# Layernorm, attention and a routed two-expert MLP on one core: gathered rows turned by DVE from quarter loads instead of by PE, with earlier loads, a folded bias and another schedule of the sums

## The reference

```python
xn = layernorm(x)                        # x: 8 x 512 x 256, 4096 tokens of 256
scale = xn[:, ::128].reshape(8, 1024)    # four rows of the batch, a factor per key
attn = softmax((xn @ k.T) * scale) @ v   # 1024 keys, 256 wide
shared = gelu(xn @ Wfc_s + bfc_s) @ Wproj_s + bproj_s      # hidden 1024
gate = top-2 of softmax(xn @ Wr), renormalised             # 8 experts
routed = sum over the two experts of gate_e * (gelu(xn @ Wfc_e + bfc_e) @ Wproj_e + bproj_e)
out = x + attn + shared + routed
```

## Time and profile before

| | |
|---|---|
| median of 3 runs | 823.47 us (821.97 to 823.82) |
| the profiled execution | 822.49 us, of which the span of instructions is 820.6 us |
| PE busy | 777.3 us (95%) |
| DVE busy | 483.1 us (59%) |
| ACT busy | 440.5 us (54%) |
| POOL busy | 260.4 us (32%) |
| HBM traffic | 157 GB/s over the span |
| mean granted clock of PE | 0.988 of full speed |

### The profile page before, as it was taken

The page is one execution under the profiler, slowest core; times in us unless marked ns, Lnnn a source line. Parts: engine busy times, 40 slices in busy tenths (PEclk is TensorE's granted clock), DMA queues, the critical chain, the costliest instruction groups (busy, mean ns, idle before and its releaser), DMA issues.

```text
span 820.6 us, 21229 instructions
## 1 busy us (share of the span) xinstructions
PE 777.3 (95%) x7222; PEld 662.1 (81%) x7222; DVE 483.1 (59%) x1215; ACT 440.5 (54%) x845; POOL 260.4 (32%) x289
## 2 busy tenths in 40 slices
PE   4999999999999986979999999999999999999996
PEld 3888876767777665868999999989999999888885
DVE  6887858888887792653444344333444433436666
ACT  5655537665559753435655465444455554455551
POOL 5445425556656650662121111112112121110000
PEclk9999999999999997999999999999999999999999
DMA  9533222746566845444422355645454536304446
GB/s 296 193 128 104 84 73 78 259 154 232 203 209 227 332 187 193 131 135 122 158 73 65 116 174 162 203 131 161 160 167 123 191 118 205 100 26 138 125 150 213
DMA packets 65627, 129.29 MB, mean 158 GB/s; under 512 B 12256, under 2 KB 47408, under 8 KB 59168
## 3 DMA queue, kind: packets, MB, share of 16 engines
q1 hardware_dynamic: 59088, 110.77, 42.2%
q0 software_dynamic: 6480, 17.77, 5.7%
HBM read 88.39 MB, written 40.13 MB: 157 GB/s over the span
## 4 chain that ended last, share of the span: by engine, by line
PE 73%; DVE 13%; POOL 5%; issue 4%; DMA 3%; SPq 1%; DVEq 0%; ACT 0%; another core or an unknown queue 0%; POOLq 0%; ACTq 0%
PE ps_h L1321 30%; PE ps_v L1341 30%; PE ps_v L1461 5%; PE ps_h L1393 4%; POOL acc L637 3%; DVE xn L895 3%; PE ps_t L1257 2%; DVE prob L1018 2%; PE ps_t L1407 1%; DVE p_t L1032 1%; DMA tokens_y<-prob,to_i 1%; POOL slots_x L660 1%; DVE acc L1040 1%; DMA b_rows<-in_L_ffn_bfc_s_dram 1%; DVE x_t L845 1%
## 5 line engine op out<-in xcount | busy, mean ns | idle before, releaser
L944 DVE TENSOR_TENSOR h_split<-h,h_split 128x512 f16<-128x512 f32 (+1 forms) x224 | 151.5, 686 | 153.5 <-ACT h_split L751 152.8
L745 ACT ACTIVATE h<-ps_h,b_fc 128x256 f32<-128x256 f32 (+1 forms) x320 | 125.7, 443 | 181.7 <-PE ps_h L1321 181.6
L1321 PE MATMUL ps_h<-x_t,w_split 128*128 128x256 f16 (+1 forms) x1920 | 196.6, 263 | 7.3 <-DVE x_t L1134 7.3
L1321 PEld LDWEIGHTS ps_h<-x_t,w_split 128*128 128x128 f16 x1920 | 172.6, 99 | 26.0 <-issue 8.1
L1341 PE MATMUL ps_v<-w_stage,h_split 128*128 128x256 f16 x1704 | 192.6, 273 | 0.0
L1341 PEld LDWEIGHTS ps_v<-w_stage,h_split 128*128 128x128 f16 x1704 | 165.1, 98 | 18.5
L704 POOL DMA_INDIRECT tokens_y<-prob,to_i x71 | 72.0, 1015 | 309.1 <-DMA tokens_y<-prob,to_i 200.1
L751 ACT CAST h_split<-h 128x512 f16<-128x512 f32 (+1 forms) x224 | 130.7, 584 | 10.1
L745 ACT ACTIVATE h<-ps_h,b_t 128x256 f32<-128x256 f32 x128 | 53.4, 467 | 76.4 <-PE ps_h L1321 76.2
L1461 PE MATMUL ps_v<-v_split,p_t 128*128 128x256 f16 x768 | 90.9, 276 | 0.0
L1321 PE MATMUL ps_h<-x_t,w_shared 128*128 128x256 f16 x768 | 89.4, 278 | 0.0
(11 more groups left out here) (156 smaller groups left out, 665.4 us busy)
## 6 DMA issues: line engine op xcount, KB each, us to landing
w_split<-wpack SPq DMA_DIRECT2D x17, 1024.0 KB, 5.3
w_stage<-wpack SPq DMA_DIRECT2D x17, 1024.0 KB, 5.3
wpack<-w_split SPq DMA_DIRECT2D x8, 1024.0 KB
wpack<-h_split SPq DMA_DIRECT2D x8, 1024.0 KB, 5.0
y_rows<-tokens_y SPq DMA_DIRECT2D x32, 256.0 KB, 3.1
x_split<-slots_x SPq DMA_DIRECT2D x31, 258.0 KB
b_pj<-bias_e SPq DMA_DIRECT2D x40, 128.5 KB, 3.1
w_stage<-in_L_ffn_Wfc_dram SPq DMA_DIRECT2D x4, 1024.0 KB
```

The costliest lines, as they stand in the source:

```text
L745: ins = nc.scalar.activation(h32[:, hc, 0:n], ps_h[:, hc * TILE:hc * TILE + n], ACT.Gelu_apprx_tanh, bias=bias[:, hc:hc + 1], scale=1.0 / WS)
L944: ve.tensor_tensor(h_split[par][:, 1, 2 * b:2 * b + 2, 0:n], h32[:, 2 * b:2 * b + 2, 0:n], h_split[par][:, 0, 2 * b:2 * b + 2, 0:n], ALU.s ...
L1321: ins = mm(ps_h[:, hc * TILE:hc * TILE + cols], wv[:, wl, c, hc * P:(hc + 1) * P], x[:, xl * DC + c, 0:cols], start=n == 0, stop=n == 3 * ...
```

## The change

It has five parts. x_split's columns are written in another order (column 4f + k holds feature f of chunk k), by DVE's cast and subtraction through a strided view; PE's turning of the sixteen tiles reads them through the same view. In the routed stage SP loads a gathered tile in four quarters of 128 columns, each to 32 partitions (`x_quad`), and DVE turns 32x32 blocks straight into x_t (`turn_slots`); `tr2`, `tr2_first`, `copy_slots` and `keep_tail` are gone, and the routing columns come by a DMA of their own (`load_tail`). The first of these loads are issued in attention step 28, before the last packed weights are stored. The shared bias is added once to the eight expert rows at the start (b_both), and `add_bias` is gone. The lower half of the first weights' low part is made by DVE instead of POOL, and the sums are spread as five, five, five, five, four, four, four and none.

```diff
+QUADS = 4
+QW = ROW // QUADS
...
+        x_quad = [t[:, :, :].rearrange("p a n -> p (a n)")[:, 0:SUB * ROW].rearrange("p (t n) -> p t n", n=QW)
+                  for t in x_split[0:2]]
...
-        PER = QT // (SHARED - NA)
+        SUMS = (range(0, 5), range(5, 10), range(10, 15), range(15, 20), range(20, 24), range(24, 28), range(28, 32), ())
...
-            sp.dma_start(b_pj_s[:, :], bproj_s.partition_broadcast(P)).then_inc(s_bpj_in, 16)
+            sp.dma_start(b_pj_s[:, :], bproj_s.partition_broadcast(EXPERTS)).then_inc(s_bpj_in, 16)
+            sp.dma_start(b_both[:, 0:D], bproj).then_inc(s_bpj_in, 16)
...
+            def load_slots(j, par, half, first=False):
+
+                if not first:
+                    wait_ge(sp, s_xt2, j - 1)
+                r = sp.value_load(tab_x[0:1, ds(j, 1)], min_val=0, max_val=SPARE)
+                n = P if half else TILE
+                for qd in range(QUADS):
+                    src = slots_x[ds(r, n), qd * QW:(qd + 1) * QW].rearrange("(b t) f -> t b f", t=32)
+                    sp.dma_start(x_quad[par][qd * 32:(qd + 1) * 32, 0:n // 32, :], src).then_inc(s_xs_in[par], 16)
+
+            def load_tail(j, par, half, first=False):
...
-                sp.dma_start(dst, src).then_inc(s_xs_in[par], 16)
-
+                if u == 28:
+
+                    wait_ge(sp, s_table, TABLE)
+                    for par in range(2):
+                        wait_ge(sp, s_scat[par], 32 * SHARED)
+                    wait_ge(sp, s_pad, 16 * (EXPERTS + SUB))
+                    load_slots(0, 0, False, first=True)
+                    load_slots(1, 1, True, first=True)
+                    wait_ge(sp, s_bt_out, 16)
+                    for n in range(4):
+                        wait_ge(sp, s_w_out[n], 16 * (EXPERTS // 4))
+                    wait_ge(sp, s_w_out[0], 16 * (JOBS // 4))
+                    load_fc(0, 0, first=True)
+
+            wait_ge(sp, s_w_out[1], 16 * (JOBS // 4))
+            load_fc(1, 1, first=True)
...
-            wait_ge(pool, s_w0_hi[1], 1)
-            g.tensor_tensor(w_shared[0][:, 2048 + HID:], w_stage[0][:, HID:], w_shared[0][:, HID:2 * HID],
-                            ALU.subtract).then_inc(s_w0_lo[1], 1)
+            wait_ge(pool, s_bpj_in, 32)
+            g.tensor_tensor(b_both[:, 0:D], b_both[:, 0:D], b_pj_s[:, :], ALU.add).then_inc(s_bias, 1)
...
-            wait_ge(pool, s_bpj_in, 16)
-            wait_ge(pool, s_fin, QT)
-            for i in range(SHARED):
-                add_bias(i)
...
+            def x_half(i, hl):
+
+                return x_split[i % 3][:, :, 0:ROW].rearrange("p a (f h c) -> p h a c f", h=2, c=DC)[:, hl]
...
-                ve.tensor_copy(x_split[i % 3][:, :, 0:D], xn[par][:, :, :]).then_inc(s_hl, 1)
+                ve.tensor_copy(x_half(i, 0), by_quad(xn[par])).then_inc(s_hl, 1)
...
-                ve.tensor_tensor(x_split[i % 3][:, :, D:ROW], xn[par][:, :, :], x_split[i % 3][:, :, 0:D],
-                                 ALU.subtract).then_inc(s_hl, 1)
+                ve.tensor_tensor(x_half(i, 1), by_quad(xn[par]), x_half(i, 0), ALU.subtract).then_inc(s_hl, 1)
...
-            def copy_slots(j, par, n=TILE):
-                dve.wait_ge(s_tr2, j + 1)
+            def turn_slots(j, par, n=TILE):
+
+                dve.wait_ge(s_xs_in[par], nth(j, par, 16 * QUADS))
                 if not (isinstance(j, int) and j < 2):
-                    dve.wait_ge(s_to, j - 1)
-                keep_tail(par, n // P)
-                dve.wait_ge(s_mm1, BANKS * (R0 + j - 1))
-                ve.tensor_copy(x_t[:, par, :, 0:n], tr16[:, :].rearrange("p (c n) -> p c n", n=TILE)[:, :, 0:n]
-                               ).then_inc(s_xt2, 1)
+                    dve.wait_ge(s_mm1, BANKS * (R0 + j - 1))
+                ve.transpose(x_t[:, par, :, 0:n].rearrange("p c (b t) -> p b c t", t=32),
+                             x_quad[par][:, 0:n // 32, :].rearrange("p b (r c) -> p b c r", r=32)).then_inc(s_xt2, 1)
...
+                            chunk = src[:, a, 0:ROW].rearrange("p (f k) -> p k f", k=2 * DC)
+                            ins = nc.tensor.transpose(out[:, n:n + P],
+                                                      chunk[:, hl * DC + c, :], ident_h[:, :])
```

More of the change, by code:

```diff
@@ L457, in _ @@
                     load_job(2)
[L460 to L478, removed]
             def expert_of(j):
@@ new lines, in load_slots @@
+                for qd in range(QUADS):
[3 more added lines that the diff above has]
+                if not first:
+                    wait_ge(sp, s_to, j - 1)
+                r = sp.value_load(tab_x[0:1, ds(j, 1)], min_val=0, max_val=SPARE)
+                subs = 1 if half else SUB
+                sp.dma_start(tail[par][:, 0:subs, :].bitcast(f16),
+                             slots_x[ds(r, subs * P), ROW:].rearrange("(a p) d -> p a d", p=P)).then_inc(s_tail[par], 16)
@@ new lines, in _ @@
+            for u in range(QT):
+                k, phase = u // 3, u % 3
+                i = NA + 1 + k
+                if phase == 1 and i < SHARED:
+                    store_row(i)
+                if u == 0:
+                    load_job(3)
+                for n in range(JOBS):
+                    if u == lo_slot(n, 1) + 1:
+                        store_job(n)
+                        if n + 4 < JOBS:
+                            load_job(n + 4)
+                if u % 4 == 2 and u // 4 + 2 < BATCH:
+                    load_scale(u // 4 + 2)
+                if u == 25:
+                    wait_ge(sp, s_table, PAD_ROWS)
+                    for e in range(EXPERTS):
+                        first_pad = sp.value_load(tab_pad[0:1, e:e + 1], min_val=0, max_val=SPARE - P)
+                        sp.dma_start(rows(slots_x, first_pad, P), zeros[:, :, :]).then_inc(s_pad, 16)
+                if u == 28:
[10 more added lines that the diff above has]
+                    load_fc(0, 0, first=True)
@@ L540, in _, with body2 @@
-            load_fc(1, 1, first=True)
             load_pj(0, 0, first=True)
+            load_tail(0, 0, False, first=True)
             load_slots(2, 0, is_half(2))
-            def body2(j, par, slots=None):
+            def body2(j, par, slots=None, this=False):
                 if j is not LAST:
@@ L550, in body2 @@
                 load_pj(j, par, first=isinstance(j, int) and j == 1)
+                load_tail(j, par, this, first=isinstance(j, int) and j == 1)
             LAST = ROUTED - 1
-            body2(1, 1, slots=(is_half(3),))
+            body2(1, 1, slots=(is_half(3),), this=True)
             body2(2, 0, slots=(is_half(4),))
             with pairs(sp, 3, MIXED - 3) as j:
-                body2(j, 1, slots=(True,))
+                body2(j, 1, slots=(True,), this=True)
                 body2(j + 1, 0, slots=(False,))
             for j in range(MIXED - 3, MIXED + 2):
-                body2(j, j % 2, slots=(is_half(j + 2),))
+                body2(j, j % 2, slots=(is_half(j + 2),), this=is_half(j))
             with pairs(sp, MIXED + 2, ROUTED - 2) as j:
@@ L581, in _ @@
             for g in range(SHARED - NA):
-                for p in range(g * PER, (g + 1) * PER):
+                for p in SUMS[g]:
                     if p + GATHERS < QT:
@@ L1258, in transpose_rows, with transpose_quads @@
                 return ins
+            def transpose_quads(src, out=tr16):
+                for hl in range(2):
+                    for c in range(DC):
+                        for a in range(SUB):
+                            n = (hl * DC + c) * TILE + a * P
+                            chunk = src[:, a, 0:ROW].rearrange("p (f k) -> p k f", k=2 * DC)
+                            ins = nc.tensor.transpose(out[:, n:n + P],
+                                                      chunk[:, hl * DC + c, :], ident_h[:, :])
+                return ins
             def tr1(i):
@@ L1490, in _, with body2 @@
                     values(u - 1)
-            def body2(j, par, prev=False, this=False, following=False):
+            def body2(j, par, prev=False, this=False):
                 up2(j, par, this)
-                tr2(j + 1, 1 - par, following)
                 down2(j - 1, 1 - par, prev)
-            tr2(1, 1, True, first=True)
             values(QT - 1)
```

95 lines of the change are left out of this document (30 added, 65 removed).

## The result

The changed kernel takes 811.08 us (median of 4 runs, 808.71 to 812.56), the kernel before 822.72 beside it: the ratio is 0.9856, with a 95% interval of 0.9824 to 0.9888. By the ratio that is 11.8 us faster, where 41.5 were forecast, and outside the range of 777 to 797. The span fell from 820.6 to 810.8 us.

The account below looks back on a forecast made before the run. PE was taken to bound the routed stage. Gains of 13.9, 11.1, 12.7, 4.9 and 0.4 us, less 1.5, gave 41.5 off 822.49: 781.0, with the median 1.0 above, so 782 us; range 777 to 787, with rivals 777 to 797.

Parts of the forecast that it names:

- PE's turns: Routed stage: PE no longer turns gathered x, DVE's transposes replacing the turns stay hidden; 13.9 us gained.
- The seven pairs: Routed steps 5 to 19, half and full steps in pairs: 0.70 us of turns saved per pair, 4.9 us gained.
- The shared bias: Routed steps 1 to 5: without POOL's bias additions to acc, 12.7 us gained, bounds 14 and 10.
- The sums: Kernel's end: the last additions finish before PE does, so only the last eviction follows; 4.9 us gained.
- x_split in another order: DVE's cast and subtraction write, and PE reads, every fourth 16-bit element: 0.3 us a tile, 1.5 us lost in all.
- steps of four elements cost: Rival, 20%: x_split's strided passes plus 3 us before half steps cost up to 17 us, not 1.5; say 790.
- Attention's end: First routed up product starts at 310.0 instead of 320.92, since loads no longer await the packed weights' store; 11.1 us gained.
- The loads' cost: Routed stage: the gathered tiles' loads have two steps of lead; the forecast sum counted no loss for them.
- small packets crowd the queues: Rival, 12%: small load packets delay POOL's scatters, which set a routed pace of 10.7 to 11 us a step; 787 to 792.
- The start: First shared up product: moving the weights' lower half from POOL to DVE gains 0.4 us, bounds -0.5 and 1.

Follow-up runs that it names:

- both cures: Changed kernel with x_split's two DVE passes writing neighbouring pairs and two of four quarter loads per tile, from tile 3, on ScalarE's queue: 788.41 us, ratio 0.9584.
- the bias alone: Kernel before with only the shared bias folded into the routed bias rows: 811.02 us beside 820.46, ratio 0.9885.
- the order alone: Kernel before with only x_split written and read in the change's order, every fourth element: 831.14 us beside 820.46, ratio 1.0145.
- weights first: Kernel with both cures, plus the first routed tile's weights loaded ahead of the eight quarter loads at attention step 28: 782.14 us, ratio 0.9505.
- the three cures: Changed kernel with neighbouring pairs in x_split, half the quarter loads on ScalarE's queue, and first routed weights ahead of quarter loads: 782.14 us, ratio 0.9505.
- the sums alone: Kernel before with only the change's schedule of final sums: 816.50 us beside 822.24, ratio 0.993.

## Why the prediction was wrong, step by step

- **PE's turns** (13.9 us): right where PE sets the pace, 8.8 of the 9.0 us. The seven pairs gave none of their 4.9, since SP set their pace; with both cures they gave 3.1. DVE's transposes were hidden in both kinds of step; the sizes taken, 1.22 and 0.69, measured 1.24 and 0.70.
- **The shared bias** (12.7): right, 12.7, shown by the bias alone.
- **The sums** (4.9): right, 4.7. The last additions and the last eviction:

```profile
...
803.00 3.76 DVE L1233 SCALAR_TENSOR_TENSOR acc<-y_rows,gates,acc 128x256 f32<-128x256 f32 x8
...
807.78 0.42 DVE L965 SCALAR_TENSOR_TENSOR acc<-ps_v,acc 128x256 f32<-128x256 f32 x1 [0.56 <-PE ps_v L1345]
```

- **x_split in another order** (1.5 us): the step that failed first. "I take 0.3 us a tile, nearer to nothing, since the same bytes move" is no reason: bytes were not the measure. The passes cost 0.96 us a tile more, the stated upper bound of 0.95, and attention's end came 11.0 us later: 7.0 of them are shown to be the order's by the run with it alone, and of the 4.0 at the start only a part is its doing (the start loses 0.7 with the order alone and 2.5 with the bias alone). Counting half of it in attention was also too mild: the prediction counted 7 us for this price, and the order alone moved the tables by 7.7 and the whole by 11.9. PE's own reads cost next to nothing (a turn takes 218 to 219 ns in both orders, eight of them 0.64 us in place of 0.62). The rival "steps of four elements cost", with 20%, was the right mechanism and put the time at 790 when nothing else went wrong; its 3 us before half steps did not come, since the transposes there took 0.70 us. Of the two rules weighed there the Trainium skill's page "SBUF — State Buffer", "Door 1: The DMA port swizzle", did not hold for DVE's writes, and "Vector Engine (DVE) Microarchitecture Reference", on the access granule, did in its direction: neighbours are what counts. In its detail it is too strict here, since pairs of 16-bit elements, one 4-byte word, were enough, and reading 4-byte words singly cost nothing (435 and 702 ns).
- **Attention's end** (11.1): mis-sized. From the tables to the first load's issue were 1.9 us and not 0.9, eight quarter loads took 5.3 us and not about 4, so the weights went out 8.4 us after the tables in place of 6.1, and the product that waits for them started 6.7 us after the issue in place of 5.3: 7.3 us gained. The lower bound of 7 was a good one. What the sum had not at all is that the product after this wait of 4.7 us runs at the lower clock, 2.5 us; with weights first both went.
- **The loads' cost** (nothing): the step that failed most, 15 us. "The loads have two steps of lead" took the place of a sum over SP's queue. SP waited 29.2 of the 117 us before, 2.1 us in each of 14 steps, and less at a faster pace. The change adds three issues, a tail load and its table read to each step, about 2.6 us by the 0.5 us that lie between two issues in the timeline and 0.6 for a read. That is more than it had to spare (with 0.45 for a read it would be 2.5). The lead was soon used up: SP waited for PE for the last time between 350 and 360 us, and PE first stood still at 396.8, for a load of weights that SP had issued only at 393.89. All the rows for this sum were in the trace of before. No rival named it: the one nearby, "small packets crowd the queues", had the wrong resource. The same stretch, 380 to 490 us, of before and of after (packets, MB, share of 16 engines):

```profile
...
q1 hardware_dynamic: 7677, 10.99, 35.0%
...
```

```profile
...
q1 hardware_dynamic: 17172, 9.39, 33.5%
...
```

More than twice the packets, with 15% fewer bytes, take 4% less time of the engines, by the byte an eighth more; and a result's scatter landed in 2.9 us (median) where it took 3.4. It was SP's instructions: fewer of them give the time back with the same packets, and reads without any packet take more.
The Trainium skill's page "DMA: Bandwidth & Descriptors", "Issuing engines are not separate DMA queues", says that issuing from several engines saves only the sequencer's time, "which is usually small relative to the DMA itself". The first half agrees with these runs; here that time was the bound, and worth 11 us.
- **The start** (0.4): not told from nothing, as far as the weights' lower half goes. What the sum left out is the wait and the slow product at 20 us.

The kernel with the three cures takes 782.1 us, about what was forecast for the change: it lacks most of the losses that the prediction took for nothing or nearly so. That it meets the number does not make the prediction right, since none of the three is part of the change.

What stays open: the start. Between 20 and 32 us PE loses 1 to 4 us to a wait and a slow product in the changed kernel, in every variant of it, with all cures too, and with the bias alone; not in the kernel before, nor with the sums alone, and only 0.7 us, without the slow product, with the order of x_split alone. The bias's part is common to all the kernels that lose it, but which of its instructions does it was not tried. The runs of the changed kernel themselves differ, 812.6 and 812.2 us at a mean granted clock of 0.987, 810.0 and 808.7 at 0.994, and the profile is of one of the longer.

## What to carry to other kernels

An engine that only issues DMAs is a queue with a budget. Add up its instructions per step, 0.5 us an issue and 0.6 a table read in this case (which make 7.2 of the 8.9 us of a step of SP; the rest is its waits and branches, an estimate), and compare with the pace that you hope for, not with the pace that you have: a faster PE takes the slack away as the new loads do. When a wait stands in front of a weight load, look at what is issued ahead of it.

Write narrow elements in neighbouring pairs. The order in which a pass runs over its elements can be chosen apart from the layout, and here it was worth 8 us for a change of two index patterns.

## What was not expected of the hardware

- A cast of 512 elements from 32 to 16 bits, written at every fourth 16-bit place, took 763 ns against 427 in a row, the subtraction 1318 against 692; in pairs at the same places 435 and 702.
- PE reading its stationary operand with a step of four 16-bit elements: 114 ns a load against 98, and nothing on the matmul.
- A 16-bit DVE transpose of 32x32 blocks, 1024 elements a partition, read with a step of four: 1.24 us, as much as the DVE pass over 1024 elements with a float32 and a float16 input (1.22) and not quite twice the plain copy of x_t (0.68).
- Small DVE passes that last longer beside a 2.1 us pass of POOL over two tiles: 1.56 us for 8 elements (0.15 otherwise), ending at 20.54 where POOL's passes ended at 20.52, and 1.37 for 4 (0.17).
